# Two late stages of a four-layer graph network on one core: picked rows reordered among the last spline's blocks, and the Gaussian sum carried by bf16 parts

## The reference, cut to what matters

```python
gauss = exp(-0.5 * sum(diff * diff / (EPS + sigma**2), axis=-1))      # E x 3
xj = x[src] @ g                                                       # E x 96
msg = sum(xj.reshape(e, 3, 32) * gauss[:, :, None], axis=1)           # E x 32
summed = segment_sum(msg, dst, num_segments=n)
```

## Time and profile before

| | us |
|---|---|
| median of 3 runs | 6663.62 |
| lowest, highest | 6661.44, 6674.17 |
| profiled execution, its own time | 6661.12 |
| span of its instructions | 6659.3 |
| TensorE matmul busy in the span | 4881.0 |
| VectorE busy | 4480.9 |
| GpSimd busy | 4088.7 |
| ScalarE busy | 1826.4 |
| mean granted TensorE clock | 0.917 |

### The profile page before, as it was taken

How to read it: one execution, slowest core, us unless ns; L and a number is a source line. 1 busy time by engine, 2 the same in 40 slices (tenths; PEclk the granted TensorE clock), 3 DMA queues, 4 the chain that set the end, 5 groups by cost and what they waited for, 6 DMA issues and landing times. The chain is left out here.

```text
span 6659.3 us, 106073 instructions
## 1 busy us (share of the span) xinstructions
PE 4881.0 (73%) x34619; PEld 3665.0 (55%) x34619; DVE 4480.9 (67%) x11674; ACT 1826.4 (27%) x3144; POOL 4088.7 (61%) x4097
## 2 busy tenths in 40 slices
PE   5444444676638888888884667999999488888885
PEld 4444444455526666666662434555555366666664
DVE  7555555469957777777771315777776687877775
ACT  1222221458824444444440000000000133333332
POOL 1777777210047777777754254777775577767773
PEclk9999999989969989999996788999999799999997
DMA  4222221123332222222226582111111211111110
GB/s 73 79 78 78 78 78 55 24 57 158 160 85 57 56 56 56 55 55 56 56 47 208 201 262 70 38 37 37 37 37 32 28 21 19 20 19 20 19 20 13
DMA packets 389292, 438.88 MB, mean 66 GB/s; under 512 B 245539, under 2 KB 313104, under 8 KB 388765
## 3 DMA queue, kind: packets, MB, share of 16 engines
q1 hardware_dynamic: 202041, 289.96, 13.9%
q0 software_dynamic: 130592, 126.27, 11.2%
q10 hardware_dynamic: 56528, 21.19, 1.6%
HBM read 355.32 MB, written 82.34 MB: 66 GB/s over the span
## 5 line engine op out<-in xcount | busy, mean ns | idle before, releaser
L967 POOL DMA_INDIRECT at_far<-att_table,at_rec x1184 | 1198.7, 1012 | 759.1 <-DMA at_rec<-rec_r 398.6
L1680 POOL DMA_INDIRECT p_far<-table,p_rec x962 | 964.6, 1003 | 455.5 <-issue 284.9
L2487 PE MATMUL g_l_ps_sum<-g_l_row,g_l_of 128*128 128x392 f32 x3224 | 1063.4, 493 | 19.4 <-DVE g_l_of L2438 19.4
L2409 POOL DMA_INDIRECT g_l_got<-table,g_l_index x806 | 811.6, 1007 | 245.5 <-issue 228.1
L550 POOL DMA_INDIRECT rec_r<-so_r_rec,so_r_place x806 | 788.1, 978 | 245.5 <-issue 245.2
L2487 PEld LDWEIGHTS g_l_ps_sum<-g_l_row,g_l_of 128*128 128x128 f32 x3224 | 614.2, 191 | 469.2 <-DVE g_l_of L2438 20.5
L505 PE MATMUL so_r_look<-so_r_table,so_r_lo_t 128*128 128x26 f32 x1612 | 425.0, 434 | 313.1 <-DVE so_r_table L447 313.1
L2421 DVE TENSOR_SCALAR g_l_row<-g_l_iota,edge_row 128x784 f32<-128x784 f32 x806 | 500.6, 694 | 224.1 <-PE g_l_ps_sum L2487 223.9
L1398 DVE TENSOR_TENSOR p_spread<-at_far,p_mask 128x256 f32<-128x256 f32 x1184 | 444.3, 422 | 299.0 <-PE at_bank L1457 290.8
L1512 ACT COPY p_outer<-at_bank 125x512 f32<-125x512 f32 x1184 | 584.4, 779 | 62.8 <-PE at_bank L1457 62.8
L505 PEld LDWEIGHTS so_r_look<-so_r_table,so_r_lo_t 128*128 128x128 f32 x1612 | 417.5, 356 | 319.6 <-DVE so_r_table L447 165.0
(11 more groups left out here) (492 smaller groups left out, 6679.0 us busy)
## 6 DMA issues: line engine op xcount, KB each, us to landing
adjacent<-ad_by_chunk SPq DMA_DIRECT2D x74, 800.0 KB, 3.3
so_r_row<-pad_src SPq DMA_DIRECT2D x62, 832.0 KB, 6.1
g_l_counts<-adjacent SPq DMA_DIRECT2D x60, 800.0 KB, 7.0
g_l1d_counts<-adjacent SPq DMA_DIRECT2D x59, 800.0 KB, 7.2
so_r_low<-pad_lo_src SPq DMA_DIRECT2D x62, 416.0 KB, 4.5
at_far<-att_table,at_rec POOLq DMA_INDIRECT x1184
p_far<-table,p_rec POOLq DMA_INDIRECT x962
rec_r<-so_r_rec,so_r_place POOLq DMA_INDIRECT x806
```

Of the source, the lines that this page charges most:

```text
L967: pool.indirect_dma_start(out=far[b][:, t, :], out_offset=None, in_=g.att_table[:, :], in_offset=bass.IndirectOffsetOnAxis(ap=rec[b][:, t, ...
L1680: pool.indirect_dma_start(out=sl.far[b][:, t, :], out_offset=None, in_=table[:, :], in_offset=bass.IndirectOffsetOnAxis(ap=sl.rec[b][:, t, ...
L2409: pool.indirect_dma_start(out=got[b][:, j, :], out_offset=None, in_=table[:, :], in_offset=bass.IndirectOffsetOnAxis(ap=index[b][:, j:j + ...
L2487: last = nc.tensor.matmul(ps_sum[k][:], of4[b][:, j, :, :].rearrange("p k f -> p (k f)"), row1[b][:, j, k * COLS:(k + 1) * COLS], start=Fa ...
```

## The change

In the last spline three things move. In `outer_products` the shifts of the next block are computed in front of tile 16. In VectorE's `following`, each half of the basis is followed by the keeping of a picked pair, pair 0 behind the first half, pair 1 behind the second; both stood behind the scan. In TensorE's `step`, pick 2 goes in front of `turn`.

```diff
-    def points(self, dve, ch, m, b, turn, first=False):
+    def points(self, dve, ch, m, b, turn, first=False, halves=range(2)):
...
+            if next_shifts is not None and t == self.HT:
+
+                self.near_shifts(pe, m + 1, *next_shifts)
...
                 def following(n, b, turn, scanned=True, keep=True, hots=True):
-                    sl.points(dve, ch, n, b, turn, first=not scanned)
+                    sl.points(dve, ch, n, b, turn, first=not scanned, halves=())
+                    for k in range(2):
+
+                        sl.make_basis(dve, n, (k,), first=not scanned)
+                        if keep:
+                            picks.keep_own(dve, ch, n + 1, k, sl.far[(b + 1) % R])
                     sl.spread(dve, n, b, first)
                     if scanned:
                         sl.scan(dve, ch, n - 1)
-                    if keep:
-                        for j in pairs[:-1]:
-                            picks.keep_own(dve, ch, n + 1, j, sl.far[(b + 1) % R])
...
-                    sl.outer_products(pe, n)
+                    sl.outer_products(pe, n, next_shifts=(nxt, turn) if nxt is not None else None)
                     if ahead:
                         picks.turn(pe, n + 2, 0)
-                    if nxt is not None:
-                        sl.near_shifts(pe, n + 1, nxt, turn)
                     sl.through_weights(pe, n)
                     if ahead:
                         for j in pairs[:-1]:
                             picks.turn(pe, n + 2, j + 1)
                             picks.pick(pe, n + 2, j)
+                        picks.pick(pe, n + 2, pairs[-1])
                     sl.turn(pe, n)
-                    if ahead:
-                        picks.pick(pe, n + 2, pairs[-1])
```

```diff
+        of4 = ps("of4", [P, HB, 4, F])
+        part = [[sb(f"part{b}{k}", [P, HB, 4, F], BF16) for k in range(3)] for b in two]
+        row1 = [sb(f"row1{b}", [P, HB, TALL], BF16) for b in two]
...
+                def one(step, b, turn, first=False, last_pair=False):
+                    if not first:
+
+                        dve.wait_ge(summed, step - 1)
+                        dve.wait_ge(parted, step)
+                    mix(step, b, turn)
+                    if not last_pair:
+                        index_of(step + 2, b)
+                    one_hots(step, b, range(by_dve // 2))
+
+                    dve.wait_ge(cut, step * 2 + 1)
+                    for at, end in pieces:
+                        here = nc.vector.tensor_sub(of4[:, at:end], of4[:, at:end], part[b][0][:, at:end])
+                    here.then_inc(rest, 1)
+                    one_hots(step, b, range(by_dve // 2, by_dve))
+                    ch.wait()
+
+                    dve.wait_ge(cut, step * 2 + 2)
+                    for at, end in pieces:
+                        here = nc.vector.tensor_sub(part[b][2][:, at:end], of4[:, at:end], part[b][1][:, at:end])
+                    here.then_inc(parted, 1)
...
-                        pe.wait_ge(ready, i * 2 + (b + 1))
+                        pe.wait_ge(parted, i * 2 + (b + 1))
+                        pe.wait_ge(hots, i * 8 + (4 * b + 4))
                         for j in range(HB):
-                            for k in two:
-                                last = nc.tensor.matmul(ps_sum[k][:], of4[b][:, j, :, :].rearrange("p k f -> p (k f)"),
-                                                        row1[b][:, j, k * COLS:(k + 1) * COLS], start=False, stop=False)
+                            for of in part[b]:
+                                for k in two:
+                                    last = nc.tensor.matmul(ps_sum[k][:], of[:, j, :, :].rearrange("p k f -> p (k f)"),
+                                                            row1[b][:, j, k * COLS:(k + 1) * COLS], start=False, stop=False)
...
+                def one_hots(step, b, js):
+                    for j in js:
+
+                        act.wait_ge(hots, step * 4 + (j - by_dve))
+                        nc.scalar.activation(apart[:], iota[:], ACT.Abs, bias=g.edge_row[:, bass.ds(step * HB + j, 1)], scale=-1.0).then_inc(aparts, 1)
+                        act.wait_ge(aparts, step * 4 + (j - by_dve + 1))
+                        nc.scalar.activation(row1[b][:, j, :], apart[:], ACT.Relu, bias=g.ones[:, 0:1], scale=-1.0).then_inc(hots, 1)
+
+                def one(step, b, first=False):
+                    if not first:
+
+                        act.wait_ge(summed, step - 1)
+                    one_hots(step, b, range(by_dve, by_dve + 2))
+                    act.wait_ge(ready, step + 1)
+                    nc.scalar.copy(part[b][0][:], of4[:]).then_inc(cut, 1)
+                    one_hots(step, b, range(by_dve + 2, HB))
+                    act.wait_ge(rest, step + 1)
+                    nc.scalar.copy(part[b][1][:], of4[:]).then_inc(cut, 1)
```

More of the change, by code:

```diff
@@ L1360, in points, with make_basis @@
             ch.wait()
-        for k in range(2):
+        self.make_basis(dve, m, halves, first)
+        if self.fin == 1:
+            ch.step(nc.vector.tensor_scalar(far[:, :, 0], self.rec[b][:, :, 0], float(N), None, ALU.is_lt))
+            ch.step(nc.vector.tensor_mul(self.third[:], v[:, :, 2, :], far[:].to_broadcast([P, TB, 5])))
+    def make_basis(self, dve, m, halves, first=False):
+        nc, v = self.nc, self.up[:].rearrange("p (t d) k -> p t d k", d=3)
+        for k in halves:
             if k == 1 or not first:
@@ L1430, in near_shifts, with outer_products @@
                               self.shift[b][:].rearrange("c t d -> c (t d)"), start=True, stop=True).then_inc(self.shifts, 1)
-    def outer_products(self, pe, m, third=None):
+    def outer_products(self, pe, m, third=None, next_shifts=None):
         ring = len(self.ps_outer)
@@ L2388, in stage_messages @@
         got = [sb(f"got{b}", [P, HB, 3 * F]) for b in two]
-        mixed = sb("mixed", [P, HB, F])
-        of4 = [sb(f"of4{b}", [P, HB, 4, F]) for b in two]
-        row1 = [sb(f"row1{b}", [P, HB, TALL]) for b in two]
+        of4 = ps("of4", [P, HB, 4, F])
+        part = [[sb(f"part{b}{k}", [P, HB, 4, F], BF16) for k in range(3)] for b in two]
+        row1 = [sb(f"row1{b}", [P, HB, TALL], BF16) for b in two]
+        apart = sb("apart", [P, TALL])
+        by_dve = HB - 4
         sums, turned_rows = sb("sums", [P, WIDE]), sb("turned_rows", [P, chunks, P])
@@ L2394, in stage_messages @@
         ps_turn = [ps(f"ps_turn{k}", [P, 4, P]) for k in two]
+        mixed = ps_turn[0][:].rearrange("p q c -> p (q c)")[:, 0:HB * F].rearrange("p (t f) -> p t f", f=F)
         gathered = [rows_sem(nc, f"{name}_gathered{b}") for b in two]
+        cut, rest, parted, hots, aparts = (sem(n) for n in ("cut", "rest", "parted", "hots", "aparts"))
         iotas, steps, indexed, mixes, ready, summed, all_in, copied, turned, out, stored, taken = (
@@ L2417, in index_of @@
                     nc.vector.tensor_copy(index[b][:], g.edge_src[:, bass.ds(step * HB, HB)]).then_inc(indexed, 1)
-                def one_hots(step, b):
-                    for j in range(HB):
+                def one_hots(step, b, js):
+                    for j in js:
                         last = nc.vector.tensor_scalar(row1[b][:, j, :], iota[:], g.edge_row[:, bass.ds(step * HB + j, 1)], None, ALU.is_equal)
                     ch.put(last)
+                pieces = ((0, 4), (4, 8), (8, HB))
                 def mix(step, b, turn):
@@ L2428, in mix @@
                     rows3 = got[b][:].rearrange("p t (k f) -> p t k f", k=3)
-                    for at, end in ((0, 5), (5, 9), (9, HB)):
+                    for at in range(0, HB, 3):
+                        end = min(at + 3, HB)
                         here = bass.ds(step * HB + at, end - at)
@@ L2433, in mix @@
                     ch.wait()
-                    ch.step(nc.vector.tensor_add(mixed[:], rows3[:, :, 0, :], rows3[:, :, 1, :]))
-                    ch.step(nc.vector.tensor_add(mixed[:], mixed[:], rows3[:, :, 2, :]))
-                    for at, end in ((0, 5), (5, 9), (9, HB)):
+                    for half in (slice(0, 6), slice(6, HB)):
+                        ch.put(nc.vector.tensor_add(mixed[:, half], rows3[:, half, 0, :], rows3[:, half, 1, :]))
+                    ch.wait()
+                    ch.step(nc.vector.tensor_add(mixed, mixed, rows3[:, :, 2, :]))
+                    for at, end in pieces:
                         b4, here = [P, end - at, 4, F], bass.ds(step * HB + at, end - at)
-                        last = nc.vector.tensor_mul(of4[b][:, at:end, :, :], mixed[:, at:end, :].unsqueeze(2).to_broadcast(b4),
+                        last = nc.vector.tensor_mul(of4[:, at:end, :, :], mixed[:, at:end, :].unsqueeze(2).to_broadcast(b4),
                                                     g.edge_of4[:, here, :].unsqueeze(3).to_broadcast(b4))
                     last.then_inc(ready, 1)
+                def one(step, b, turn, first=False, last_pair=False):
```

(24 more changed lines are left out.)

3 lines of the change are left out of this document (removed).

## The result

| | median us | ratio to before | 95% interval |
|---|---|---|---|
| before, 9 runs | 6664.8 | | |
| changed, 9 runs | 6643.99 (6639.5 to 6656.56) | 0.9969 | 0.996 to 0.9977 |

The change makes the kernel 0.31% faster, some 21 us. The forecast was no change at 6666 us. The measured time lies in its range, but a gain of 13 us and more had been given a chance of only 0.35.

A forecast was written before the change was run, and what follows sets the result against it. Gaussian stage: TensorE at 17.15 us a step, GpSimd 0.1 below; spline: a ring of VectorE and TensorE waiting in turn, 36.7 us a block. Gaussian -7 and spline +11 made +4 us: 6666 us, range 6612 to 6694.

The forecast's parts named there:

- The bound of the Gaussian stage: Gaussian stage before: TensorE binds at 17.15 us a step, GpSimd 0.1 below; 0.30 us idle before each gather is no slack.
- TensorE, VectorE, ScalarE a step: Changed Gaussian stage: TensorE 13.1 us, VectorE 15.3, ScalarE 11.8 a step, all under GpSimd, which sets the step.
- the rival in which VectorE binds: Gaussian stage: bf16 one-hots cost 0.98 us each, VectorE 18.6 us a step, +90, about 6760 us; chance 0.08.
- The 0.1 us for a further piece: VectorE's other Gaussian work: each of three more pieces costs 0.1 us, taken from between 0 and 0.26.
- I take 995 ns, slightly under the 1003 and 1007 of the two stages: Gaussian stage: mean time of a gather after the change, giving -0.16 us a step, -10 us.
- the rule: VectorE instructions with two SBUF inputs lock the port pair shared with GpSimd; with a PSUM input, gathers come near their floor.
- The bound from above: Gaussian stage: gathers slowed by VectorE take at most 1.04 us each, 17.5 us a step.
- a rival at 0.19 with a price of -53: Gaussian gathers at their floor, each disturbance gone: -53, +3 at the end, +11 in the spline, 6622 us; chance 0.19.
- The end of the stage: Behind the last Gaussian gather: 29.5 us grow to 30.6 plus up to 2.3 of clock, +2 to 3 us.
- The spline: Per block: products earlier -2.4, shifts +0.4, clock loss moved from pick 2 to outer products +2.3: +0.3 us, +11 in all.
- D: Spline: the moment VectorE ends its last spread step; outer products at D + 23.4 before, predicted at D + 21.0.
- The sum: Gaussian stage -7 and spline +11 make +4 us on the profiled 6661.12: 6666 us, no change; chance 0.40.

The follow-up runs named there:

- before_mixed: Kernel before with one Gaussian-stage tile, the sums over the three kernels, in PSUM instead of SBUF; 6665.81 us, ratio 1.0004.
- spline_only: Last spline as changed, Gaussian stage as in the kernel before; 6675.69 us, ratio 1.0020.
- gauss_keeps2: Changed kernel with the next shifts back where they were; keeping behind the basis halves and pair 2 in front of turning stay; 6648.43 us, ratio 0.9976.
- gauss_sbuf: Like gauss_only, but the f32 tiles of the spread products and of the two sums lie in SBUF instead of PSUM; 6655.65 us, ratio 0.9988.
- gauss_only: Gaussian stage as changed, last spline as in the kernel before; 6627.10 us, ratio 0.9949.
- after_filled2: Changed kernel plus 64 transposes in front of turning that compute nothing and fill TensorE's idle stretch; 6591.74 us, ratio 0.9895.
- gauss_filled: gauss_only plus 64 empty transposes in front of turning, behind a wait for ScalarE's last copy; 6620.83 us, ratio 0.9925.

## Why the prediction was wrong

- **The bound of the Gaussian stage: right.** GpSimd 0.1 us a step under TensorE, its idle 0.30 us no slack; before_mixed shows the one bound, the changed kernel the other.
- **TensorE, VectorE, ScalarE a step: right.** 13.1 us were worked out and 13.1 measured; VectorE's 15.3 are 4729.48 - 4712.85 - 1.73 = 14.9; ScalarE's 11.8 are 8 x 0.95 + 1.55 + 1.53 = 10.7; none binds. The one-hots in bf16 come every 0.62 us (2.46/4), so the rival in which VectorE binds fell. The 0.1 us for a further piece was chosen from a span that mixes a mean of 548 ns with a busy time of 643; with busy time on both sides the rows give 0.10, so the choice was right by luck.
- **The step that failed: "I take 995 ns, slightly under the 1003 and 1007 of the two stages".** It was 963. This term was given -10 us and brought -35. The rows of the kernel before were asked for a mean of other stages, and not which instructions stand beside a held-up gather; that trace had 120 of its 175 beside the sums and the spreading. The place where it was weighed against the rule, "the many undisturbed ones do not", took undisturbed gathers beside one-hots, which read one tile and a single column, for evidence against it. That place also gave the first sum an input in PSUM; it only writes there (L2434 in before_mixed, L2449 in the changed kernel), and gathers beside it are still held up. The bound from above, worked out again from its own terms, is 1.05 us and not 1.04. The case was a rival at 0.19 with a price of -53; -35 is two thirds of the way.
- **The end of the stage: right.** +2 to 3 us, measured 31.9 - 29.4 = +2.5; the clock that it reckoned with did fall there, the last step's 78 matmuls took 15.9 us.
- **The spline: right.** +0.3 us a block and +11 in all, measured +0.4, +14, and +13.5 in spline_only; with the wait of 1.5 us for pick 0 (1.61), the idle stretch of 4.6 (4.46), pick 2 at full speed and the loss moved to the outer products (+2.9 us on 16 tiles). Two sizes were off and cancelled, so the total is in part luck: the loss was put at 2.3, and the products start at 5840.10 in the trace, D + 20.5 and not D + 21.0, so -2.9 + 0.4 + 2.9 = +0.4. That the period of the changed kernel is so steady was not foreseen: most of its blocks, and those of gauss_keeps2, are 37.4 to 37.7 us long, while most blocks before varied from 35.8 to 37.6. In spline_only they go 35.6, 37.5 and 39.5 in turn, with the same mean.
- **The sum.** With 963 for 995 the same working gives -33 + 11 = -22: 6639 on the profiled execution's 6661, 6642 with the 2.5 us to the median, and 6644 was measured.

## What to carry to other kernels

Before pricing GpSimd's share of a change, list which VectorE instructions stand beside the longer gathers: sources moved to PSUM were worth 28 us here, and only with TensorE's matmuls shortened too: one such source alone, in the kernel before, was worth nothing. When a change removes a wait, ask what the other moves put in its place; here one of three moves alone was worth 108 us, and the two others together took it back. The timeline has 5.4 us of work and waiting that they put in front of the scan; that this is the reason is argued from it, not shown by a run. An idle stretch of TensorE in a ring costs twice, once as idle time and once as low clock behind it, and where the low stretch falls decides its price.

## What the runs showed of the hardware

- A gather that GpSimd issues takes 944 ns undisturbed and up to some 1.4 us beside VectorE's work. The Trainium skill, "SBUF — State Buffer", section "SBUF: two separate sides", names VectorE's instructions with two SBUF inputs among those that take the port pair shared with GpSimd, against an instruction of GpSimd that reads SBUF; the gathers read their indices there. The runs agree for the sources (gauss_sbuf 997 ns, gauss_only 961; L2434 with two SBUF sources still holds gathers up in before_mixed). An exclusive lock for the whole instruction they do not show: in the kernel before, of 247 gathers beside instructions with two SBUF sources 120 took 990 ns or more, and the others no longer than undisturbed ones. Nor are such instructions the only ones beside held-up gathers: 54 of the 384 beside one-hots alone, which read one tile and a single column, were held up too.
- An index copy of 13 columns on VectorE took 293 ns in the kernel before and 165 in before_mixed. The source of the instruction in front of it does not explain that: in gauss_sbuf the median is 168 behind one with two sources in SBUF.
- TensorE's granted clock fell to the level of 1.2 GHz behind an idle stretch of 4.5 us, within one of 6.0 us, and behind one of 2.1 us (pick 2 at 4.36 us). With the filler it did not fall behind stretches of 0.9 us (after_filled2); behind 1.1 to 1.4 us (gauss_filled) pick 2 was slow in 15 blocks of 35.
- A loop of TensorE with 192 more transposes a turn stood still at its return, ten times for 3.4 to 3.7 us in after_filled2 and ten times for 1.4 to 3.4 us in gauss_filled; those without them did not.
